# Cross-attention output product of a decoder kernel: one four-pass product of normalised contexts, replaced by three one-pass products of high and low parts that start before the last softmax sums

## The reference, cut to what matters

```python
B, T, C = 4, 256, 256;  H = 16;  L = 1601;  D = 64        # D: latent width of keys and values
scores = einsum('bhsr,bhlr->bhsl', q_r, k_r)              # 16 heads, 256 queries, 1601 keys
attn   = softmax(scores, axis=-1)
ctx_c  = einsum('bhsl,bld->bhsd', attn, kv_r)             # context of a head: 256 x 64
ctx_lat = einsum('bhsd,hkd->bhsk', ctx_c, w_kc_kv)
x = x + ctx_lat.transpose(0, 2, 1, 3).reshape(B, S, H*K) @ Wo.T
# then layernorm(x), router logits, top-1 expert, capacity 160, expert products w1, gelu, w2
```

## Time and profile before

| | us |
|---|---|
| median of 3 runs | 1382.12 (1380.94 to 1385.76) |
| the profiled execution | 1389.93, its span 1388.1 |
| busy in the span: PE, DVE, ACT, POOL | 1267.8, 812.3, 616.7, 820.8 |
| the loop over the 32 units | from about 229 to 730.5 |
| output products | 734.0 to 765.0 |

### The profile page before, as it was taken

The page is one execution under the profiler, slowest core; times in us unless marked ns, Lnnn a source line. Parts: engine busy times, 40 slices in busy tenths (PEclk is TensorE's granted clock), DMA queues, the critical chain, the costliest instruction groups (busy, mean ns, idle before and its releaser), DMA issues.

```text
span 1388.1 us, 20144 instructions
## 1 busy us (share of the span) xinstructions
PE 1267.8 (91%) x7051; PEld 824.3 (59%) x7051; DVE 812.3 (59%) x1444; ACT 616.7 (44%) x1644; POOL 820.8 (59%) x747
## 2 busy tenths in 40 slices
PE   7999998999999999999988576998999998989792
PEld 4865545666666666666657563444777884547582
DVE  5756666666766667666733626776666214764443
ACT  4731113544444444445440323888766025872151
POOL 1266005999999999999990534888544003660444
PEclk9999997999999999999998786999999999998897
DMA  8501110000000000000008320000000105200263
GB/s 259 134 9 38 31 38 19 9 9 12 9 9 9 8 13 9 9 9 9 12 1 276 86 80 27 0 1 1 1 1 1 27 0 154 62 2 31 69 141 118
DMA packets 67532, 60.12 MB, mean 43 GB/s; under 512 B 19440, under 2 KB 64392, under 8 KB 66920
## 3 DMA queue, kind: packets, MB, share of 16 engines
q1 hardware_dynamic: 64408, 50.56, 13.2%
q0 software_dynamic: 3024, 8.26, 2.5%
HBM read 40.58 MB, written 9.83 MB: 36 GB/s over the span
## 4 chain that ended last, share of the span: by engine, by line
PE 76%; POOL 7%; DVE 6%; ACT 6%; issue 3%; DMA 1%; another core or an unknown queue 0%; POOLq 0%; DVEq 0%; SPq 0%; ACTq 0%
PE PS L481 71%; PE PS L489 4%; ACT s_sc L1300 2%; POOL PWS L1934 2%; POOL a_m L1994 2%; POOL a_m L1988 2%; DVE s_mx L1719 1%; ACT a_m L1257 1%; DVE HN L1402 1%; POOL slot_rows L1974 1%; DVE pm L1511 1%; PE PS L638 1%; PE PS L675 0%; DVE stats L1392 0%
## 5 line engine op out<-in xcount | busy, mean ns | idle before, releaser
L1934 POOL TENSOR_TENSOR PWS<-PWS 128x1024 f32<-128x1024 f32 x160 | 379.2, 2370 | 46.1 <-ACT PWS L1196 26.8
L1511 DVE TENSOR_REDUCE pm<-PS 128x2 f32<-128x1024 f32 x192 | 226.1, 1221 | 106.4 <-PE PS L481 106.3
L1196 ACT ACTIVATE PWS<-PS 128x512 f32<-128x512 f32 (+1 forms) x416 | 212.7, 600 | 79.0 <-PE PS L481 73.9
L481 PE MATMUL PS<-PWS,KVR 128*64 128x256 f32 (+1 forms) x1664 | 185.2, 379 | 0.0
L481 PE MATMUL PS<-QALL,KH 128*128 128x512 f32 (+1 forms) x416 | 181.3, 436 | 0.1
L481 PE MATMUL PS<-QM,KL 68*128 68x512 f32 (+1 forms) x416 | 166.1, 399 | 0.0
L2009 POOL TENSOR_SCALAR s_sc<-s_sc,s_ri 128x128 f32<-128x128 f32 (+1 forms) x256 | 103.9, 425 | 93.4 <-DVE s_ri L1726 93.4
L481 PEld LDWEIGHTS PS<-PWS,KVR 128*64 128x64 f32 (+1 forms) x1664 | 121.4, 137 | 58.2 <-issue 0.2
L481 PEld LDWEIGHTS PS<-QALL,KH 128*128 128x128 f32 (+1 forms) x416 | 77.1, 185 | 76.7 <-ACT PWS L1196 58.9
L1300 ACT ACTIVATE s_sc<-PS,s_nb 128x128 f32<-128x128 f32 (+1 forms) x256 | 104.6, 434 | 4.5 <-DVE s_nb L1722 4.5
L1202 ACT ACTIVATE CTX<-PS 128x256 f32<-128x256 f32 x32 | 12.3, 385 | 194.5 <-PE PS L481 194.5
(11 more groups left out here) (307 smaller groups left out, 2377.2 us busy)
## 6 DMA issues: line engine op xcount, KB each, us to landing
QALL<-qlo SPq DMA_DIRECT2D x32, 128.0 KB, 2.4
QM<-QALL SPq DMA_DIRECT2D x64, 64.0 KB, 2.0
f_w<-in_L_ffn_w_dram SPq DMA_DIRECT2D x2, 2048.0 KB
tile_results<-e_y SPq DMA_DIRECT2D x31, 128.0 KB
a_nat<-in_L_attn_w_qkv_dram SPq DMA_DIRECT2D x1, 3072.0 KB, 22.0
x_wq<-in_L_xattn_Wq_dram SPq DMA_DIRECT2D x1, 2048.0 KB, 10.4
x_wo<-in_L_xattn_Wo_dram SPq DMA_DIRECT2D x2, 1024.0 KB, 7.4
a_wo<-in_L_attn_w_o_dram SPq DMA_DIRECT2D x1, 2048.0 KB, 21.1
```

Source lines behind the costliest of these rows:

```text
L481: return nc.tensor.matmul(o, a, b, start=start, stop=stop, **kw)
L1196: nc.scalar.activation(PW[c][0:rows, j * HALF:(j + 1) * HALF], st_bank("block", LT * u + lt)[0:rows, :], ACT.Exp).then_inc(p_ready, 1)
L1511: V.tensor_reduce(pm[u % 2][:, :, i // 3, i % 3], src, AX, ALU.max).then_inc(nat_read, 1)
L1934: G.tensor_tensor(ACC[:, :], PW[0][:, :] if i == 0 else ACC[:, :], PW[i + 1][:, :], ALU.add).then_inc(acc_step, 1)
```

## The change

- `attended(t)` is a `split_product` of 24 one-pass products (3 for each pair): stationary high part of the context, moving high part of `U`; high, low; low, high. The high parts lie in places of `QALL` that are no longer read, the low parts over `CTX` in place (`CTXL`) and in `UL`.
- ACT makes the high parts: `high_part(u - 1)` in unit `u`, between its exponentials and `context_out(u)`; in the last 8 units also one of the 8 of `U`.
- DVE makes the low parts right behind `normalised(u - 1)`, in the last 8 units also one of `U`, ahead of the maxima that close the unit.
- The meeting of the four engines behind the loop goes; each only drains and counts, and SP still waits for all four. PE starts the products of tiles 0 and 1 right behind the last context, ahead of the last `weight_sums`; DVE scales and splits the last unit between its tiles 1 and 2.
- A PSUM bank's number is now counted from a given start (`start_at(3)`): tile 0 takes bank 3.
- The experts' weights `f_w1`, `f_w2` are loaded behind the store of the cleared slots, with a semaphore of their own that the first expert product waits for; before, the router stage waited for them.

```diff
@@ class PsumBanks
+        self.base, self.first = 0, 0
+
+    def start_at(self, bank):
+        self.base, self.first = len(self.order), bank
...
+        self.jobs[key] = (len(self.order), by, self.count[by], (self.first + len(self.order) - self.base) % 8,
+                          self.order[-8] if len(self.order) - self.base >= 8 else None)
@@ names
+        CTXL = at("CTXL", 151744, [P, PAIRS, B * T], F32R)
+        UL = at("UL", 184576, [P, PAIRS, C], F32R)
...
+        def context_high(b, p):
+            return QALL[:, p % 4, b, p // 4, :]
+        def weights_high(p):
+            return QALL[:, 6, p // 2, p % 2, :] if p < 6 else QALL[:, 7, 0, p % 2, :]
+        SPLIT_FROM = 2 * PAIRS + 8
@@ PE
-            weight_sums(UNITS - 1)
-            ended(pe, 3)
+            pe.drain().then_inc(phase_ended, 1)
+            banks.start_at(3)
             def attended(t):
-                out_product(("xo", t), [(CTX[:, p, t * P:(t + 1) * P], U[:, p, :]) for p in range(PAIRS)])
+                if t == 0:
+                    pe.wait_ge(nat_read, PLAINS * UNITS)
+                if t == 4:
+                    pe.wait_ge(ctx_read, UNITS)
+                pe.wait_ge(cl_ready, PAIRS * (t // 2 + 1))
+                if t >= 5:
+                    pe.wait_ge(norm_done, UNITS)
+                if t == 0:
+                    pe.wait_ge(ul_ready, PAIRS)
+                b, at_ = t // 2, t % 2 * P
+                ps = begin(("xo", t), "dve")
+                split_product(ps[:, 0:C], [(context_high(b, p)[:, at_:at_ + P], CTXL[:, p, t * P:(t + 1) * P],
+                                            weights_high(p), UL[:, p, :]) for p in range(PAIRS)]).then_inc(filled, 1)
...
+                if e == 0:
+                    pe.wait_ge(experts_loaded, 32)
...
-            for t in range(6):
+            for t in range(2):
+                attended(t)
+            weight_sums(UNITS - 1)
+            for t in range(2, 6):
                 attended(t)
             turn_half(0)
             attended(6)
-            pe.wait_ge(moe0_loaded, 16 * 5)
+            pe.wait_ge(moe0_loaded, 16 * 3)
@@ ACT
+            def high_part(u):
+                b, p = divmod(u, PAIRS)
+                act.wait_ge(norm_done, u + 1)
+                nc.scalar.activation(context_high(b, p), CTX[:, p, b * T:(b + 1) * T], ACT.Copy).then_inc(ch_ready, 1)
+            def weights_high_part(p):
+                nc.scalar.activation(weights_high(p), U[:, p, :], ACT.Copy).then_inc(uh_ready, 1)
...
+                if u >= 1:
+                    high_part(u - 1)
+                if 0 <= u - SPLIT_FROM < PAIRS:
+                    weights_high_part(u - SPLIT_FROM)
                 context_out(u)
-            ended(act, 3)
+            act.drain().then_inc(phase_ended, 1)
+            high_part(UNITS - 1)
@@ DVE
+            def low_part(u):
+                b, p = divmod(u, PAIRS)
+                dve.wait_ge(ch_ready, u + 1)
+                V.tensor_tensor(CTXL[:, p, b * T:(b + 1) * T], CTX[:, p, b * T:(b + 1) * T], context_high(b, p).bitcast(F32),
+                                ALU.subtract).then_inc(cl_ready, 1)
+            def weights_low_part(p):
+                dve.wait_ge(uh_ready, p + 1)
+                V.tensor_tensor(UL[:, p, :], U[:, p, :], weights_high(p).bitcast(F32), ALU.subtract).then_inc(ul_ready, 1)
...
                 if u >= 1:
                     normalised(u - 1)
+                    low_part(u - 1)
+                if 0 <= u - SPLIT_FROM < PAIRS:
+                    weights_low_part(u - SPLIT_FROM)
                 for n in after:
                     maxima(n)
-            normalised(UNITS - 1)
-            ended(dve, 3)
+            dve.drain().then_inc(phase_ended, 1)
             def attended(t):
+                if t == 2:
+                    normalised(UNITS - 1)
+                    low_part(UNITS - 1)
@@ POOL
-            ended(pool, 3)
+            pool.drain().then_inc(phase_ended, 1)
@@ SP
-            sp.dma_start(f_w1[:, :, :, :], L0_ffn_w1.rearrange("e (k p) i -> p e k i", p=P)).then_inc(moe0_loaded, 16)
-            sp.dma_start(f_w2[:, :, :, :], L0_ffn_w2.rearrange("e (k p) i -> p e k i", p=P)).then_inc(moe0_loaded, 16)
...
             sp.dma_start(xs0.rearrange("(j p) c -> p j c", p=P), f_xg[:, :, :]).then_inc(slots_zeroed, 16)
+            sp.dma_start(f_w1[:, :, :, :], L0_ffn_w1.rearrange("e (k p) i -> p e k i", p=P)).then_inc(experts_loaded, 16)
+            sp.dma_start(f_w2[:, :, :, :], L0_ffn_w2.rearrange("e (k p) i -> p e k i", p=P)).then_inc(experts_loaded, 16)
```

More of the change, by code:

```diff
@@ L57, in claim @@
         self.count[by] += 1
-        self.jobs[key] = (len(self.order), by, self.count[by])
+        self.jobs[key] = (len(self.order), by, self.count[by], (self.first + len(self.order) - self.base) % 8,
+                          self.order[-8] if len(self.order) - self.base >= 8 else None)
         self.order.append(key)
@@ L62, in bank @@
     def bank(self, key):
-        n = self.jobs[key][0] % 8
+        n = self.jobs[key][3]
         return self.psum[:, n * 512:(n + 1) * 512]
     def earlier(self, key):
-        n = self.jobs[key][0]
-        return self.order[n - 8] if n >= 8 else None
+        return self.jobs[key][4]
     def filled(self, key):
@@ L73, in emptied @@
     def emptied(self, key):
-        _, by, n = self.jobs[key]
+        by, n = self.jobs[key][1:3]
         return self.emptied_sem[by], n
@@ L78, in take @@
         self.taken[by] += 1
-        assert self.jobs[key][1:] == (by, self.taken[by]), (key, self.jobs[key], self.taken)
+        assert self.jobs[key][1:3] == (by, self.taken[by]), (key, self.jobs[key], self.taken)
         return self.bank(key)
@@ L384, in decoder @@
         norm_done = sem("context_normalised")
+        ch_ready = sem("context_high_parts")
+        cl_ready = sem("context_low_parts")
+        uh_ready = sem("output_weights_high_parts")
+        ul_ready = sem("output_weights_low_parts")
+        experts_loaded = sem("moe0_expert_weights_loaded")
+        inv_ready = sem("weight_sums_inverted")
         mask_ready = sem("expert_choice_ready")
@@ L1543, in normalised @@
                 sums = st_bank("sums", u)[:, 0:T]
-                link(V.reciprocal(sums, sums))
+                V.reciprocal(sums, sums).then_inc(inv_ready, 1)
+                dve.wait_ge(inv_ready, u + 1)
                 dve.wait_ge(ctx_read, u + 1)
@@ L1597, in first_choice @@
                 link(V.tensor_tensor(dst[:, tiles, 0:E], v, bcast(f_mx[:, 3, tiles], E), ALU.is_equal))
-            dve.wait_ge(moe0_loaded, 16 * 5)
+            dve.wait_ge(moe0_loaded, 16 * 3)
             link(V.memset(f_pre[:, 0, :], 0.0))
```

## The result

| | before | changed |
|---|---|---|
| median, us (lowest to highest) | 1383.94 (1380.94 to 1385.82) | 1367.82 (1365.50 to 1370.18) |
| the profiled execution, its span | 1389.93, 1388.1 | 1368.55, 1366.8 |

The changed kernel takes 0.9868 of the time before, 95% interval 0.9841 to 0.9895: 16.1 us of the medians (forecast 9, to 1373, range 1365 to 1382). A later comparison gave 0.9880 (0.9832 to 0.9927).

What follows compares the result with a forecast made beforehand. The prediction took PE to bound the loop, POOL close behind. Early start and one-pass products gain 15.1 us, POOL's later end takes 6.1, leaving 9.0: 1382.1 to 1373.1 us, range 1365 to 1382.

Steps and rivals of the forecast that it cites:

- The start: Behind the loop: without the meeting and with one-pass products, tile 7 comes 15.1 us earlier, if the loop ends as before.
- The products: Output product: 24 one-pass instructions at 0.12 us each make a tile in 2.88 us in place of 3.46.
- The rival of 0.227: Output product: one-pass products cost as much as those of 512 columns, 0.227 us; 5 us slower, 1387; chance 0.05.
- The subtractions are held: Loop: DVE's subtractions with both operands in SBUF wait for POOL's add, up to 2.37 + 0.42 us each.
- Rival 1: Loop: subtractions are not held, POOL ends at 730.5 and the whole 15.1 us comes, 1367; chance 0.25.
- Each takes 0.42 from POOL, less some of the 0.12: Loop: 39 subtractions cost POOL 0.39 us each, 15.2 in all; less 9.1 idle, POOL ends 6.1 later.
- rival 3: Loop: POOL pays more per subtraction than its work; at 0.9 us each 11 us slower, 1393; chance 0.08.
- The range: Whole kernel: 1365 to 1382 us, taking in the unheld case and half of the PE stall, leaving out slower rivals.
- The forecast's own bounds for one subtraction: Loop: POOL loses 0.30 to 0.54 us a subtraction and ends 2.6 to 12.0 later, 1370 to 1379.
- rival 2: Last 8 units: the held second subtraction stalls PE; 4 us gained, 1378, or 1389 at the worst; chance 0.12.
- The loads: Behind tile 7: the experts' weights land 25.8 us after it, PE needs them 36.2 after it; cost nothing.
- The sum: Whole kernel: 15.1 us gained less POOL's 6.1 is 9.0, so the median goes from 1382.1 to 1373.1.

Runs made afterwards that it cites:

- experiment 1: The changed kernel without any splitting: early start kept, old two-pass products, no subtractions; 1370.48 us against 1387.96 for the kernel before, ratio 0.9903.
- experiment 3: The changed kernel with the last sums ahead of tile 0, still without a meeting; 1378.55 us against 1387.96 for the kernel before, ratio 0.9936.
- experiment 4: The changed kernel with the context's low part subtracted from a scaled value in PSUM, not SBUF; 1369.83 us against 1387.96 for the kernel before, ratio 0.9880.
- experiment 2: The changed kernel with the meeting, last sums and last unit's splitting back ahead of tile 0; 1385.66 us against 1387.96 for the kernel before, ratio 0.9981.
- experiment 5: The changed kernel with each context subtraction but the last made twice, first into an unused place; 1395.93 us against 1395.22 for the kernel before, ratio 0.9992.
- experiment 6: The changed kernel with the 8 splittings of U one unit earlier, none in the last; 1381.03 us against 1395.22 for the kernel before, ratio 0.9895.

## Why the prediction came out as it did

- **The start** was right: predicted 15.1 with the products, of which experiment 1 shows 10.3 for the start alone (10.7 by the prediction's terms), experiment 3 that it hangs on the two tiles ahead of POOL's last add, and the kernel of experiment 4, where PE does not wait for a held subtraction, 15.2 with the products. The 1.3 us that the gain at tile 7 lacks are the wait for `U`, 1.0, and 0.4 lost in the last 8 units. Full clock throughout, as forecast.
- **The products** were right: 2.82 us a tile for 2.88, 0.117 for 0.12. The rival of 0.227 is out. What PE gains by them is 5.0 us over eight tiles at full clock, and 4.2 where it had paused (experiment 2).
- **The subtractions are held** was right, and for the reason given: 1516 ns as median with both operands in SBUF, 425 with one in PSUM. Rival 1 took the right size of the gain for a wrong reason: it had 15.1 because nothing would be held.
- **"Each takes 0.42 from POOL, less some of the 0.12"** is the step that failed. The term was 0.39 each, 15.2 us, with 0.30 as its lower bound; measured it is 2.1 to 2.9 us for 39, 0.05 to 0.07 each, and 0.05 in the doubled kernel. That POOL gives way is not refuted: experiment 5 has adds that grow by 0.12 to 0.14 where a subtraction runs into them for 0.27. What the term left out is how little of a held subtraction reaches POOL's next add. It took off 0.03, part of the hand-over, while 0.14 lie beside the end of the add in front, 0.08 in the hand-over and 0.14 in the first part of the next add. The trace before had a sign of it, used only against rival 3: the two adds beside the held L1709 followed each other without a gap. So POOL's last add ended 0.35 us later against its last add of the first unit (485.99 for 485.64), not 6.1; the rest of the 2.8 came out of its idle time. The forecast of 9.0 was 5 too small.
- **The range** held by luck in this: the time of 1367.8 lies in it because it took in the first rival. The forecast's own bounds for one subtraction, 0.30 to 0.54, gave 1370 to 1379 and missed.
- **A wait the prediction did not have**: PE for the last low part of `U`, 1.3 us, 1.0 more than it is idle there without it. The held pair of subtractions was priced in the units in the middle, where DVE has idle time, and not in the last, where PE asks for the result itself.
- **The second subtraction** (rival 2) cost 0.4 us in the last 8 units, against at most 22. One more of them in each unit cost 12.5, of which waits for maxima name 4.0: the cover was nearly used up.
- **The loads**: nothing late. The experts' weights are asked for 36.1 us behind tile 7 (789.30 against 753.21; forecast 36.2) and PE does not wait.
- **The sum**: 13.8 at tile 7. The medians' 16.1 is this and about 2 us that no stretch touched by the change shows.

## What to carry to other kernels

When two engines share SBUF, price the one that is held, and price it by where its result is next asked for; charge the other only for what runs on into its next instruction (here 0.07 us of 0.42). Taking one operand from PSUM took the hold away (1.47 us to 0.43), and it need not cost an instruction. Independent work that needs none of the late engine's data belongs ahead of the product that waits for it; it keeps PE's clock up as well.

## What the runs showed of the hardware

- DVE with both operands in SBUF ends 0.28 to 0.34 us behind the end of the POOL add that ran when it started. POOL's next instruction starts 0.08 or 0.14 us behind the last all the same, and loses 0.05 to 0.07 us on average; it loses 0.12 to 0.14 where the subtraction runs into it for 0.27. The Trainium skill (SBUF — State Buffer, SBUF: two separate sides) has each wait for the whole of the other. The runs agree for DVE, in 39 of 39 cases. For POOL they show a small price that grows with what the subtraction has left, which fits such a wait behind a start-up of some 0.14 us; whether POOL stands still for that time no record shows.
- One-pass products of 256 columns are 0.117 us apart at full clock and 0.213 at the lower level, which was granted behind an idle PE of 6 us (experiment 3) and of 3.9 us (experiment 5).
- One kernel on one chip can differ by 18 us between executions (that of experiment 6: 1373.5 to 1391.4), and the changed kernel's two profiles differ by 19, in stretches that can be named. The length of a stretch between two events of the trace told 1 us apart, where the intervals of the ratios are 4 to 14 us wide.
